# A feed-forward kernel on eight cores: the second layernorm's last two vector operations on separate steps, the output stored from the scratch tile, and the next tile loaded through two queues

## The reference

```python
x = x + layernorm(attention(layernorm(x)))            # only the last 516 rows attend
x = x + layernorm(ffn(layernorm(x)))

def ffn(x):                                           # dim 1024, hidden 4096, rank 16
    h = bitlinear(x, w_fc) + gate * (x @ v.T @ fast_b.T @ u.T)
    r = maximum(h, 0.0)
    return bitlinear(r * r, w_proj)                   # x is 2 x 16384 x 1024 in all
```

## Time and profile before

| | |
|---|---|
| time before, median of 2 runs | 2784.92 us (2780.18 to 2789.67) |
| the profiled execution | 2793.15 us |
| its span on the slowest core (core 7) | 2791.6 us |
| spans of the 8 cores | 2771.7 to 2791.6 us |
| mean granted TensorE clock, 8 cores | 0.706 to 0.721 |
| feed-forward stage on core 7 | from 1404 us to the end |
| DMA traffic in the whole run | 80.50 MB, mean 29 GB/s |

### The profile page before, as it was taken

One profiled execution on the slowest core, in us unless ns is written; L12 is line 12 of the kernel. 1 busy time (PEld: TensorE's weight loads), 2 busy tenths in 40 slices (PEclk: granted clock), 3 DMA queues, 4 the chain that ended last, 5 costly groups with the idle time before them and its releaser, 6 DMA issues.

```text
span 2791.6 us, 31660 instructions; the slowest of 8 cores (2771.7 to 2791.6 us)
## 1 busy us (share of the span) xinstructions
PE 1636.3 (59%) x10824; PEld 1073.1 (38%) x10824; DVE 1325.2 (47%) x2281; ACT 479.4 (17%) x1025; POOL 8.8 (0%) x20
## 2 busy tenths in 40 slices
PE   2333333323333333333668878888887888887886
PEld 0111111101111111111146656666666666666665
DVE  1145554554544454545645444454444544444544
ACT  1111111111111111111011211112112111111121
POOL 0000000000000000000000000000000000000000
PEclk7555555555555555555579999989999999999898
DMA  2101011101000100011010011100001100111000
GB/s 43 31 23 45 30 48 35 46 30 45 31 23 30 38 31 23 23 30 31 15 31 15 17 31 31 31 18 14 31 31 31 31 13 19 31 31 31 18 14 31
DMA packets 55086, 80.50 MB, mean 29 GB/s; under 512 B 11763, under 2 KB 45684, under 8 KB 53892
## 3 DMA queue, kind: packets, MB, share of 16 engines
q1 hardware_dynamic: 36436, 52.99, 6.4%
q10 hardware_dynamic: 16640, 16.78, 1.9%
q0 software_dynamic: 1856, 8.72, 1.7%
HBM read 70.42 MB, written 16.78 MB: 31 GB/s over the span
## 4 chain that ended last, share of the span: by engine, by line
PE 45%; DVE 29%; issue 9%; DMA 8%; ACT 8%; DVEq 1%; ACTq 0%; SPq 0%; POOLq 0%
PE pb L109 45%; DVE lnscr L109 7%; DVE srowp L109 5%; DVE stg L109 4%; DVE srow L109 4%; DMA xtl<-xT 3%; ACT sgn L109 3%; DMA outT<-xtl 3%; DMA ctxXg<-ctxT 2%; DVE xtl L109 1%; ACT srow L109 1%; ACT lnscr L109 1%; DVE r2s L109 1%; DVE sgn L109 1%; DVE fsq L109 1%
## 5 line engine op out<-in xcount | busy, mean ns | idle before, releaser
L109 PE MATMUL pb<-xn,Sfc 128*128 128x256 bf16 x4096 | 563.3, 284 | 119.5 <-DVE r2s L109 113.3
L109 PE MATMUL pb<-r2s,Spj 128*128 128x256 bf16 x4096 | 558.1, 286 | 0.0
L109 PEld LDWEIGHTS pb<-xn,Sfc 128*128 128x128 bf16 x4096 | 409.9, 102 | 209.1 <-issue 146.7
L109 PEld LDWEIGHTS pb<-r2s,Spj 128*128 128x128 bf16 x4096 | 414.2, 102 | 93.5 <-issue 29.6
L109 DVE TENSOR_TENSOR r2s<-pb,rpp 128x256 bf16<-128x256 f32 x512 | 215.6, 424 | 481.3 <-ACT rpp L109 425.2
L109 PE MATMUL pb<-sgn,cvecb 128*1 128x512 bf16 x256 | 129.5, 609 | 430.0 <-DVE lnscr L109 430.0
L109 DVE SCALAR_TENSOR_TENSOR lnscr<-stg,sgn 128x1024 bf16<-128x1024 f32 x128 | 156.6, 1223 | 296.5 <-ACT sgn L109 296.5
L109 ACT ACTIVATE rpp<-pb,hsc 128x256 f32<-128x256 f32 x256 | 122.2, 477 | 937.9 <-PE pb L109 799.9
L109 PE MATMUL pb<-lnscr,cvecb 128*1 128x512 bf16 x472 | 206.6, 566 | 76.5 <-ACT lnscr L109 75.7
L109 PEld LDWEIGHTS pb<-sgn,cvecb 128*1 128x1 bf16 x256 | 14.5, 80 | 494.7 <-issue 494.7
L109 DVE TENSOR_TENSOR stg<-stg,pb 128x1024 f32<-128x1024 f32 (+1 forms) x96 | 151.1, 1574 | 96.9 <-ACT hsc L109 56.4
(11 more groups left out here) (101 smaller groups left out, 1193.7 us busy)
## 6 DMA issues: line engine op xcount, KB each, us to landing
stg<-wfc_st SPq DMA_DIRECT2D x32, 512.0 KB, 3.7
stg<-wpj_st SPq DMA_DIRECT2D x32, 512.0 KB, 3.7
xtl<-xT SPq DMA_DIRECT2D x16, 1024.0 KB, 6.2
outT<-xtl ACTq DMA_DIRECT2D x16, 1024.0 KB, 5.3
ctxXg<-ctxT SPq DMA_DIRECT2D x8, 256.0 KB, 3.2
wbuf<-wk POOLq DMA_DIRECT2D x2, 1024.0 KB, 12.2
wbuf<-wq POOLq DMA_DIRECT2D x2, 1024.0 KB, 9.6
wbuf<-wv POOLq DMA_DIRECT2D x2, 1024.0 KB, 9.7
```

What stands on the lines that cost most here:

```text
L109: inst = getattr(engobj, fname)(*args, **kwargs)
```

## The change

Four edits, all in the feed-forward stage, and a helper.

1. In the tail of the second layernorm the subtract is emitted at step 13 and the rest (`ln2_tail`) at step 15. The add writes `fscr` in place of `xtl`, and the store reads `fscr`. So `xtl` is free at the add's end, and `fscr` when the store has completed.
2. The load of the next tile is emitted at step 15 and waits for the add alone. It is split: feature blocks 0 to 3 by SP as before, blocks 4 to 7 by GpSimd, with a semaphore of its own. Whoever waits for a load waits for both.
3. The first layernorm's subtract is emitted at step 29, one step behind its multiply, and no longer after the loop.
4. Guard waits that two engines need are given to both (`gwait2`); before, the second `gwait` of the same key found nothing.

```diff
+    def gwait2(self, engs, key):
+        for sem, val in self.guards.pop(key, []):
+            for e in engs:
+                self.wait(e, sem, val)
...
                 if cast_split:
+                    E.gwait2(("scalar", "vector"), scr_key)
...
-                    E.gwait("vector", scr_key)
...
-                E.gwait("sync", f"xtl{j % 2}")
-                xload[j] = E.dma("sync", v3(xtl[j % 2], TT),
-                                 t_x[:, j * TT:(j + 1) * TT].rearrange(
-                                     "(c p) t -> p c t", p=128), f"dS{j % 2}")
+                E.gwait2(("sync", "gpsimd"), f"xtl{j % 2}")
+                xv = v3(xtl[j % 2], TT)
+                ca = E.dma("sync", xv[:, 0:4, :],
+                           t_x[0:512, j * TT:(j + 1) * TT].rearrange(
+                               "(c p) t -> p c t", p=128), f"dS{j % 2}")
+                cb = E.dma("gpsimd", xv[:, 4:8, :],
+                           t_x[512:1024, j * TT:(j + 1) * TT].rearrange(
+                               "(c p) t -> p c t", p=128),
+                           "dGi" if j % 2 == 0 else "dM")
+                xload[j] = (ca, cb)
...
             def ln2_tail(p, g2):
-                adv(g2)
                 xfp3 = v3(xtl[p % 2], TT)
                 E.drain("vector")
-                E.op("vector", "tensor_tensor", xfp3, xfp3, fscr3, ALU.add,
+                E.op("vector", "tensor_tensor", fscr3, xfp3, fscr3, ALU.add,
                      inc="sV")
                 cOut = E.cnt["sV"]
-                E.gset("fscr", "sV")
+                E.gset(f"xtl{p % 2}", "sV")
                 E.drain("vector")
                 E.wait("scalar", "sV", cOut)
                 cS = E.dma("scalar",
                            t_out[:, p * TT:(p + 1) * TT].rearrange(
-                               "(c p) t -> p c t", p=128), xfp3, f"dO{p % 2}")
+                               "(c p) t -> p c t", p=128), fscr3, f"dO{p % 2}")
                 c_store.append((f"dO{p % 2}", cS))
-                E.gset(f"xtl{p % 2}", f"dO{p % 2}")
+                E.gset("fscr", f"dO{p % 2}")
...
                         elif hc == 13:
+                            adv(pend2)
+                        elif hc == 15:
                             ln2_tail(j - 1, pend2)
                             pend2 = None
-                    if hc == 13 and j >= 1:
+                    if hc == 15 and j >= 1:
                         emit_xload(j + 1)
...
                         elif hc == 28:
                             adv(ln1[0])
+                        elif hc == 29:
+                            adv(ln1[0])
+                            E.gset("fscr", "sV")
+                            tile_state[j + 1] = ln1[1][0]
                 E.gset(f"xn{j % 2}", "sP")
-                if j + 1 < n_tiles:
-                    adv(ln1[0])
-                    E.gset("fscr", "sV")
-                    tile_state[j + 1] = ln1[1][0]
...
-                E.gwait("scalar", "fsq")
-                E.gwait("scalar", "fscr")
+                E.gwait2(("scalar", "vector"), "fsq")
+                E.gwait2(("scalar", "vector"), "fscr")
```

More of the change, by code:

```diff
@@ L194, in emit_ln_gen @@
                     E.wait("scalar", sem, val)
-                E.gwait("scalar", scr_key)
                 if cast_split:
+                    E.gwait2(("scalar", "vector"), scr_key)
                     E.op("scalar", "activation", scr3[:, 0:4, 0:W],
@@ L210, in emit_ln_gen @@
                 else:
+                    E.gwait("scalar", scr_key)
                     E.op("scalar", "activation", scr3[:, :, 0:W], src3,
@@ L925, in emit_xload @@
                     E.wait("sync", "sV", c_attn)
+                    E.wait("gpsimd", "sV", c_attn)
                 if j < 2:
                     E.wait("sync", f"dS{j % 2}", E.cnt[f"dS{j % 2}"])
-                E.gwait("sync", f"xtl{j % 2}")
-                xload[j] = E.dma("sync", v3(xtl[j % 2], TT),
-                                 t_x[:, j * TT:(j + 1) * TT].rearrange(
-                                     "(c p) t -> p c t", p=128), f"dS{j % 2}")
+                E.gwait2(("sync", "gpsimd"), f"xtl{j % 2}")
[8 more added lines that the diff above has]
+                xload[j] = (ca, cb)
             emit_xload(0)
@@ L941, in ln1_start @@
                 if jj == n_tiles - 1 and n_tiles == NTILE:
-                    E.wait("vector", f"dS{jj % 2}", xload[jj])
+                    E.wait("vector", f"dS{jj % 2}", xload[jj][0])
+                    E.wait("vector", "dGi" if jj % 2 == 0 else "dM",
+                           xload[jj][1])
                     E.wait("vector", "sV", c_attn)
@@ L950, in ln1_start @@
                 g = emit_ln_gen(xfj3, xn3_t[jj % 2], TT,
-                                src_wait=[(f"dS{jj % 2}", xload[jj])]
+                                src_wait=[(f"dS{jj % 2}", xload[jj][0]),
+                                          ("dGi" if jj % 2 == 0 else "dM",
+                                           xload[jj][1])]
                                 + merge_wait,
@@ L1110, in build_nc @@
                 E.gset("pbproj1", "sA")
-                E.gwait("vector", "fsq")
-                E.gwait("vector", "fscr")
                 E.wait("vector", "sP", c_proj)
```

## The result

| | before | changed |
|---|---|---|
| median | 2785.74 us (37 runs) | 2796.27 us (38 runs) |
| ratio of the times | 1 | 1.0032, 95% interval 1.0019 to 1.0044 |
| the profiled execution | 2793.15 us | 2783.67 us |
| its span (core 7 in both) | 2791.6 us | 2782.1 us |

A forecast was written before the change was run, and what follows sets the result against it. PE was taken as the bound where fed, with two waits per tile on one chain. 14 us won, 9 lost to the clock and 3 from the last tile gave 8 us faster, 2,777 us; range 2,748 to 2,812.

The forecast's parts named there:

- S + 19.5: Kernel before: PE restarts after its second wait 19.5 us after the second layernorm's subtract starts on DVE.
- L - E: Time from the end of the second layernorm's add to the next tile's casts on DVE; 11.8 us before the change.
- the chain: Subtract, add, store and load, casts, PE's restart in each tile; PE time saved inside it is worth nothing.
- S + 18.5: Changed kernel: PE restarts after its second wait 18.5 us after the subtract's start, 1.0 us before the old restart.
- D: Time for store and load together, 2 MB, after the add in the changed kernel: 9.4 us, ends 8.7 and 11.1.
- The first wait 1.4 to 1.6 us: PE's wait for `r2s` after the second layernorm's add, 1.4 to 1.6 us in place of 3.5.
- The last tile's 3 us: No load follows in the last tile, so its shorter first wait counts: 3 us saved once.
- The clock, 0.65 us a tile: Slow matmuls at 1.2 GHz behind PE's second wait: 0.65 us more per tile, 9 us over 14 tiles.
- rival D: GpSimd's half load is late, its work standing behind a DVE operation: 24 us slower, 2,809 us; chance 0.10.
- Rival E: Store and load run beside each other at their own speeds, 6.4 us: 50 us won, 2,735 us; chance 0.10.
- Rival C: Store and load contend, 11.1 us together after the add: 16 us slower, 2,801 us; chance 0.18.
- The sum: Over 14 tiles 14 us won, clock takes back 9, last tile gives 3: 8 us won, median 2,777 us.

The follow-up runs named there:

- e8: Kernel before with only the tail divided: subtract at step 13, add, store and load at 15; ratio 1.0145 to the kernel before, 40 us slower.
- e2: Changed kernel with subtract, add, store and load all at step 13; ratio 0.9891 to the kernel before, 30 us faster.
- e3: Changed kernel with the load as one transfer by SP, the store still beside it; ratio 1.0055 to the kernel before.
- e9: Changed kernel with both halves of the load issued by SP, a semaphore each, nothing by GpSimd; ratio 1.0018 to the kernel before.

## Why the prediction was wrong

- **The restart of the kernel before at S + 19.5: wrong, the step that failed.** Its 11.8 us for L - E was the mean of 14 tiles of one core, and that the slowest of its execution. Core 7 was the slowest there partly because its transfers were late: 0.7 us a tile more than the mean of that execution, 10 of the 12 us by which it lay above the mean core. All eight cores give 11.0, so the restart lies at S + 18.7, and the chain gained 0.2 us a tile, not 1.0: 3 us over 14 tiles in place of 14.
- **The restart of the changed kernel at S + 18.5: right,** term by term: 6.0 (6.1 foreseen), 9.5 (9.4), 3.0. That D came out so close is partly luck. Of its two sources the loads at the start had been read on all cores, but with a slip: the second load is issued 0.47 us after the first, so core 4 gives 8.3 and not 8.8, core 7 gives 11.0, and the mean is 9.5. The other source, 9.3, is made of core 7's transfers; those of all cores in the two executions give about 9.0 (10.8 one after the other, less the 1.8 of a 4.8 us store that are not data).
- **The first wait 1.4 to 1.6 us: right** (1.45), as was its being worth nothing inside the chain (e8).
- **The last tile's 3 us: right.** From the last subtract to the end it took 65.9 us before and 62.5 after, in the mean of the cores.
- **The clock, 0.65 us a tile: too small, for the same reason.** Its old value, 1.55, was core 7's again; the mean of the cores is 1.0. The new one, 2.2, was about right (2.0, in every tile of every core). So the slow matmuls behind the casts rose by 1.0 us. Those elsewhere fell by about 0.6, which no step of the prediction has and which was not explained, and those inside the chain (1.0 to 0) count for nothing. The kernel before had its slow matmuls around the chain half covered by the transfers, the changed kernel has them all in the open. That this is a cost of the divided tail, e2 and e8 show.
- **No loss from GpSimd's queue, rival D: right that it doesn't decide.** GpSimd's half and the store land together (8.8 and 8.8). GpSimd issues 0.48 us behind SP and takes 0.75 us for it, in all 14 tiles of all cores. No run here shows the lock of which the Trainium skill tells ("SBUF — State Buffer", the box on DVE blocking DMA in "SBUF: two separate sides"); the operations behind the add read PSUM.
- **Rival E, each transfer at its own speed: out.** 5.3 and 5.8 us became 8.8 and 8.8. The Trainium skill's statement that transfers of all queues interleave on the same engines ("DMA: Bandwidth & Descriptors", "Issuing engines are not separate DMA queues") agrees with that; how the load was cut and queued moved the store's landing between 8.8 and 9.7 us, and the time by 0.1 to 0.4%, which the intervals hardly tell from nothing.
- **Rival C, contention with D at 11.1: not the reason,** though its time of 2,801 is nearer than the forecast's 2,777; D was 9.5.
- **The sum.** With 11.0 in place of 11.8 the forecast's own terms give 3 - 9 + 3 = 3 us slower instead of 8 faster; with the clock's 1.0 in place of 0.65 it is 8 slower, and the 0.6 elsewhere takes that back. The profiled executions show no change per tile (84.6 and 84.5), the timed ones 0.3 to 0.4% slower. Of that the scatter of the cores is a part that no step of the sum held: it summed one core and never asked how the maximum of eight would move. So the lost gain of the chain is explained, and the last 9 us only in part.

## What to carry to other kernels

Where two waits lie on one chain, shortening the first by moving its work later lengthened the second by more (2.1 us less, 2.9 more); look first for what stands in front of the engine's queue while it waits (here casts for the next tile, four steps too early), and move that. Read a term that a change replaces on all cores, not on the slowest: the slowest core is the slowest because some terms are longest there. When a wait goes from one place to another, ask whether the slow matmuls behind it fall under cover or into the open.

## What the runs showed of the hardware

- A 1 MB store and a 1 MB load in flight together land after 9.7 and 8.0 us (two queues, e3) or 8.8 and 8.8 (load halved, three queues), alone after 4.4 to 5.3 and 5.4 to 6.8 by core: together 9.4 to 9.8 us from the add's end, one behind the other 11.0.
- Issued within 0.01 us of each other, a store and a load in one transfer did not land together: in e3 the load landed 1.7 us before the store by core 0's medians, 1.1 in the mean of all cores. With the load in halves (changed, e9) the later half and the store landed within half a microsecond of each other.
- A stretch at half clock stood behind every second wait of over 3 us in the changed kernel (2.0 us a tile lost), and behind none of under 1 us in the kernel before. In e2, where the second wait is 0.5 us in the mean, 0.3 us a tile were lost.
